# Gating the gathers of a graph-attention stage by four columns where it was two

## The reference

```
gl = (x @ W_l).reshape(n, 6, 64);  gr = (x @ W_r).reshape(n, 6, 64)
e  = einsum('ehf,hf->eh', leaky_relu(gl[src] + gr[dst], 0.2), att)
p  = exp(e - segment_max(e, dst)[dst])
alpha = p / (segment_sum(p, dst)[dst] + 1e-16)
out = selu(segment_sum(alpha[:, :, None] * gl[src], dst).mean(axis=1) + bias)
x   = layernorm(x + out)
```

## Time and profile before

| engine | busy us of 5765.2 | of the span |
|---|---|---|
| TensorE | 1591.1 | 28% |
| VectorE | 2736.5 | 47% |
| ScalarE | 1757.8 | 30% |
| GpSimd | 3585.2 | 62% |

### The profile page before, as it was taken

The page is one execution under the profiler, slowest core; times in us unless marked ns, Lnnn a source line. Parts: engine busy times, 40 slices in busy tenths (PEclk is TensorE's granted clock), DMA queues, the critical chain, the costliest instruction groups (busy, mean ns, idle before and its releaser), DMA issues.

```text
span 5765.2 us, 30361 instructions
## 1 busy us (share of the span) xinstructions
PE 1591.1 (28%) x6543; PEld 800.4 (14%) x6543; DVE 2736.5 (47%) x5146; ACT 1757.8 (30%) x3826; POOL 3585.2 (62%) x3636
## 2 busy tenths in 40 slices
PE   4541111000000000000438777777783100000002
PEld 1331101000000000000213333233333100000002
DVE  1343333312344545455316677776677442644343
ACT  1111111221011212122216666676674210311111
POOL 5356556577676666674665666666535576677775
PEclk6775555555555555555669899998896555555555
DMA  4322112232122222232113444544444121322222
GB/s 131 122 63 64 51 55 65 89 96 59 45 71 60 74 69 75 60 78 65 35 45 129 172 163 168 179 161 168 150 168 136 55 63 42 103 77 67 74 67 61
DMA packets 185648, 529.56 MB, mean 92 GB/s; under 512 B 70422, under 2 KB 74626, under 8 KB 169192
## 3 DMA queue, kind: packets, MB, share of 16 engines
q1 hardware_dynamic: 65528, 395.51, 18.2%
q0 software_dynamic: 117696, 129.81, 11.2%
q10 hardware_dynamic: 2224, 2.13, 0.1%
HBM read 185.57 MB, written 341.44 MB: 91 GB/s over the span
## 4 chain that ended last, share of the span: by engine, by line
PE 13%; POOL 13%; another core or an unknown queue 10%; issue 8%; ACT 5%; DVE 3%; DMA 0%; DVEq 0%; ACTq 0%; POOLq 0%
POOL AR L191 13%; PE ps L1355 8%; PE ps L1371 2%; ACT AR L1506 2%; ACT AR L1362 2%; PE ps L1340 1%; PE ps L1386 1%; DVE AR L1520 1%; ACT AR L1379 0%; ACT AR L1347 0%; ACT AR L1796 0%; PE ps L1219 0%; DVE AR L1855 0%; DMA s<-AR 0%
## 5 line engine op out<-in xcount | busy, mean ns | idle before, releaser
L191 POOL DMA_INDIRECT AR<-xt,Si x2496 | 2468.9, 989 | 1238.5 <-issue 744.5
L191 POOL DMA_INDIRECT AR<-y,R x752 | 719.6, 957 | 545.6 <-issue 226.3
L1355 PE MATMUL ps<-AR,WLR 128*128 128x512 f32 x1248 | 688.4, 677 | 120.4 <-issue 85.5
L1520 DVE SCALAR_TENSOR_TENSOR AR<-AR,gf 128x390 f32<-128x390 f32 x780 | 484.6, 621 | 341.0 <-ACT AR L1506 240.1
L1506 ACT ACTIVATE AR<-AR 128x64 f32<-128x64 f32 x1664 | 494.7, 345 | 0.0
L1362 ACT ACTIVATE AR<-ps 128x512 f32<-128x512 f32 x624 | 369.5, 593 | 360.1 <-remote 193.5
L1837 DVE TENSOR_TENSOR AR<-AR,ps 128x2048 f32<-128x2048 f32 (+1 forms) x53 | 187.1, 3530 | 508.9 <-DMA AR<-xt,Si 508.9
L1796 ACT COPY AR<-AR 128x2048 f32<-128x2048 f32 (+1 forms) x53 | 189.3, 3572 | 725.0 <-issue 500.2
L1003 PE MATMUL ps<-AR,ones 128*128 128x128 f32 x2 | 0.8, 502 | 1334.7 <-DVE AR L988 1334.7
L1855 DVE TENSOR_TENSOR_SCAN AR<-ps,AR 128x512 f32<-128x512 f32 x208 | 242.4, 1207 | 155.8 <-issue 91.2
L191 POOL DMA_INDIRECT AR<-s,endi x196 | 216.3, 1103 | 141.1 <-issue 68.1
(11 more groups left out here) (338 smaller groups left out, 3705.7 us busy)
## 6 DMA issues: line engine op xcount, KB each, us to landing
s<-AR SPq DMA_DIRECT2D x51, 3168.0 KB
AR<-xd SPq DMA_DIRECT2D x104, 512.0 KB
s<-AR SPq DMA_DIRECT2D x51, 1024.0 KB
AR<-xt,Si POOLq DMA_INDIRECT x2496
s<-AR SPq DMA_DIRECT2D x53, 512.0 KB
s<-AR SPq DMA_DIRECT2D x51, 528.0 KB
xd<-AR SPq DMA_DIRECT2D x52, 512.0 KB
y<-AR SPq DMA_DIRECT2D x24, 1024.0 KB
```

The lines of the kernel that those rows point to most:

```text
L191: g.indirect_dma_start(out=o, out_offset=None, in_=table, in_offset=bass.IndirectOffsetOnAxis(ap=idx, axis=0)).then_inc(S[sem], 16)
L1355: t.matmul(PS[2 + k % 3][:], WLR[:, ch * P:(ch + 1) * P], XT2[:, u % 6, :], start=True, stop=True).then_inc(S["pm"], 1)
L1520: m = v.scalar_tensor_tensor(out=Sv[:, j, 0:HW], in0=Sv[:, j - 1, 0:HW], scalar=gf[:, c * CH + j:c * CH + j + 1], in1=Sv[:, j, 0:HW], op0= ...
```

## The change

In `g2_chunk` the two waits stand ahead of every fourth column, and their values are those of the last two columns of the group of four: p2 by one product more, ap by four scaled copies more. Nothing else differs; every gather has the same place in GpSimd's order.

```
             for j in range(CH):
-                if c >= NX and j % 2 == 0:
-                    e.wait_ge(S["p2"], p2_end(c - NX) - 7 + j // 2)
-                    e.wait_ge(S["ap"], 33 * (c - NX) + 1 + 2 * (j + 2))
+                if c >= NX and j % 4 == 0:
+                    e.wait_ge(S["p2"], p2_end(c - NX) - 6 + j // 2)
+                    e.wait_ge(S["ap"], 33 * (c - NX) + 1 + 2 * (j + 4))
                 gather(xsv(c)[:, j, 0:D], xt2, Si[:, c * CH + j:c * CH + j + 1], f"g_{2 * (c % NX) + j // 8}")
```

## The result

With the waits ahead of every fourth column the kernel takes 5812.77 us, the median of 11 runs (5795.04 to 5828.19), against 5771.82 us for 11 runs of the kernel before (5746.79 to 5797.72). The ratio is 1.0065, with a 95% interval of 1.0044 to 1.0086: slower by 0.65%, about 41 us. No change was forecast (5768).

What follows compares the result with a forecast made beforehand. No engine was full; layer 2's chain of waits, led by TensorE's line 1355 (35.6%), bound it, with gathers off it. Terms 0 - 0 + 0 on the profiled 5767.17 us, rounded up, gave 5768 us, range 5730 to 5811.

Steps and rivals of the forecast that it cites:

- The waits removed cost nothing: In layer 2's chunk loop, removing 188 of 376 wait pairs ahead of gathers counts 0, at most 2 us gained.
- The slack of a gather: Layer 2's gathers lead their transposes by 47.8 to 50.9 us; the change makes them 2.5 to 11.8 us later.
- Rival 3: Layer 2's transposes wait for late gathers, needing 47.8 us of delay against 11.8 found; 5768 to 5780; chance 0.02.
- GpSimd keeps up: In layer 2 GpSimd has 5.0 us free a chunk; counted 0, at worst 14 us off the lead.
- Gathers in fours: Layer 2's profile would show a gap behind each fourth gather, the three others 0.30 us apart.
- rival 4: Layer 2's stricter wait is never met first, GpSimd running behind releases; time as forecast; chance 0.58 together with the forecast.
- The end of the stage hangs on nothing moved: After layer 2's last gather TensorE still has two chunks to do, 19.2 us apart; counted 0.
- What is not in the sum: the pauses: In layer 2, 16 of 46 chunks pause, 27.27 us against 25.4; shifted gathers might matter, but nothing was added.
- Rival 1: Fewer gathers inside layer 2's pauses, so all chunks run at 25.4 us: 30 us less, 5737; chance 0.20.
- Rival 2: Gathers bunched behind a chunk's store put all layer 2 chunks in long rhythm: 56 us more, 5824; chance 0.20.

Runs made afterwards that it cites:

- first batch: Kernel before (5719.47 us) run beside waits ahead of every eighth (5783.31) or every column (5689.15), no loop gathers (5436.62), and fewer xd loads (5731.45 us).

## Why the prediction was wrong

Point by point, by its own steps.

- **The waits removed cost nothing: right.** GpSimd issues gathers 0.30 us apart whether it has passed a wait or not, after as before. With every column waiting, twice the number, the kernel was even faster.
- **The slack of a gather: right.** The last gather starts at 4312.21, and the second half of chunk 51 starts at 4356.18:

```profile
4312.21 1.03 POOL L191 DMA_INDIRECT AR<-xt,Si  x1 [0.30 <-issue]
```

```profile
4356.18 0.60 PE L1340 MATMUL ps<-ident,AR 128*128 128x128 f32 x4
```

  The lead is 44.0 us (47.8 before) and 43.4 for this chunk's first half, and in the other chunks from 5 on it is 51 to 65; 36 or more was asked. Line 1340 waits for no gather. Rival 3 is out.
- **GpSimd keeps up: right.** Its waits are 319 us against 290, so it has more free time, not less.
- **Gathers in fours: only in part.** 90 waits, where 188 gathers have a gate: half of the gates are met when GpSimd comes to them, because it runs behind its releases. That half is rival 4, and it has a consequence that I drew for no chunk: an engine that runs behind issues without a gap, so a free place always has some gather in it.
- **The end of the stage hangs on nothing moved: right.** Behind the last gathers chunks take 19.2 us, from 4336.46 to 4355.68 in TensorE's rows of line 1386.
- **"What is not in the sum: the pauses": this step failed.** I put them outside the sum, at 0, with 0.20 for each direction, because the rows of before didn't say what brings them. What stood in its place is that the pauses grew: the block went from 11.55 to 12.75 us in the mean of 44 chunks, and 37.8 of the 48.9 us between the two spans lie in layer 2. The runs put one price on all that the gathers cost: without them in the loop the time is 283 us lower in condition A, 5%, where I had given the gathers nothing on the path. The chunk goes from 26.0 to 19.5 us; of the 6.5 us, 4.0 are the block (11.55 to 7.51) and 2.5 the rest (14.43 to 11.97). Not all of it is the pauses: in condition B, where there are none, the same edit gains 71 us (4825.27 to 4753.99), since there 16 gathers bound the chunk. By this an estimate for the pauses is 283 - 71 = 212 us.
- **Rival 1's argument failed in its place.** It counted: in groups of four the sixth and seventh column would have to wait for a release behind the pause, so two gathers fewer would lie in it. The gate does move these columns, but GpSimd runs behind, and other columns, just released in a group, are issued at the same moment. The gathers in the block became more, 7.1 against 6.4, not fewer. And with the coarse release their place became fixed: about 1.0 and 2.2 us behind the last matmul in every chunk from 20 to 47, where before 11 of these 28 had a gap or another step there. That this place is what costs the 41 us is not shown: the run without xd loads has it too, at the time of the kernel before.
- **Rival 2 had the direction and the kind of growth, in less than its full form.** It gave 56 us, if all 46 chunks took the long rhythm. 26 did, not 16, and the 20 others rose from 25.4 to 26.3 us: 10 x (27.3 - 25.4) + 20 x 0.9 = 37 us, against 38.9 measured in the stretch. It named the sign from 16 more paused chunks on; with 10 the sign was already decided, since shorter forms of the pause, which I had not counted, grew too. Its reason, transfers just behind a chunk's store, was not tested by any run. The count of long distances is no measure of the pauses either: the run without xd loads has none between 27.15 and 27.45 us and a pause in every chunk.

The rule that the prediction weighed, in the Trainium skill, "Trainium Architecture — The Big Picture", section "What this means for kernel authors", says that engine lanes and DMA ports, as the two sides of the on-chip memory, cannot contend. Of the memory itself this case's rows agree: VectorE's product takes 680 or 681 ns in every run here, with gathers or without, and in condition B the block is 7.5 us with five gathers in it or none. As a reason to count a transfer off the path at zero it did not serve: in condition A the block is 11.55 us with gathers and 7.51 without. What is late there, by the recorded updates of the semaphores, is a signal.

**Shown and not shown.** Shown in condition A: there are no pauses in layer 2's loop without gathers and there are without xd loads, so gathers are needed for them; in the pauses TensorE's updates of its semaphores are recorded 1 to 6 us behind its work; and the width of the group orders the time, in four kernels and two repeats, with four columns and the others in different batches. Shown: no effect of the change in condition B, where no trace has a pause. Only argued: why a wider group makes the block longer. The place just behind the block's last matmul was my reading, and two runs speak against it as the whole cause: the one without xd loads has gathers there in every chunk and is no slower, and with eight columns most holds lie ahead of that place and the blocks are the longest. The two pairs of kernels that moved the gathers alone fell into condition B. Only argued: that the updates come late because they stand behind those of the gathers; the gathers' completions recorded just ahead of them fit it. Whether the stores beside the gathers are needed, which of the two waits of the gate carries the effect, which part of a gather does it (its instruction, its 128 rows or the news of their landing) are open, and so is what sets the condition. It is not a property of the kernel, nor of one chip: the chip of the first batch, in A, ran the second, in B, 15 minutes later.

**A better version.** In condition A the kernel with waits ahead of every column beats both, 0.994 and 0.9958 of before. In condition B it wasn't run.

## What to carry to other kernels

A transfer with 48 us to spare can still set the time: lead is measured against its consumer, and says nothing of who else is held while it runs. Where many waits end on a releaser that the profile can't name, don't leave them out of the sum; leave the suspected transfer out in one run first, and learn what they are worth, and look up when the semaphores waited for were updated. Try releasing buffers in the smallest steps that the order allows: here that was 0.4 to 0.6% faster in condition A, and the waits saved by coarser steps were worth nothing. And run the kernel before in each batch: 41 us can't be seen beside a difference of 950 between two conditions.

## What the runs showed of the hardware

- **Two conditions of one program.** The kernel before takes 5719 to 5772 us in A and 4816 to 4825 us in B, by the medians of the batches. In A many waits of all engines end on an unknown releaser, in layer 1 as well: VectorE's scan of line 920, before, in condition A,

```profile
1705.72 0.25 DVE L920 TENSOR_TENSOR_SCAN AR<-Bn,AR 128x16 f32<-128x16 f32 x1 [2.90 <-remote]
```

  stands 2.90 us. It waits for a semaphore of VectorE's own: the product of line 918 that raises it ends at 1701.02, and the update is recorded at 1705.70, 4.7 us later. In condition B (after) the same instruction follows the one ahead of it with no idle time, and no engine waits for an unknown releaser there between 1000 and 3000 us. ScalarE's line 941 alone waits 528.4 us for it in A, before. The unknown releaser isn't another core or queue: all 563 waits put down to it in the trace of before are for semaphores that the kernel's own engines raise, with an update that is recorded over 1.5 us behind their work. That is why the difference of the conditions, 950 us, is so much larger than what layer 2 can hold.

- **A sign by which to tell them.** The row of issued gathers ends with their median time to landing in B (2.5 us, after) and with the bare count in A. The trace of A also lacks records of the engines' updates: 436 for the 624 that line 1355 makes, before, against 624 in B (after).
- **Matmul behind a pause.** After a hold of 6 us TensorE's first six matmul records of line 1355 take 4.71 us instead of 2.74, at a granted clock of half the full rate (0.50); this is 2.0 us of a chunk of 26.0.
- **A series of gathers has a price of its own**: 1.01 us each in the mean and 0.30 between, 20.9 us for 16, against a chunk of 21.0 in B, after, and of 19.5 with 8 gathers or none.
